# Second layer of a mixture of graph experts: dense over all nodes, or only over gathered (node, expert) rows

## The chip, the core and the metric

The kernel runs on one core of one Trainium2 chip. The metric is the device time of one execution in microseconds (us); smaller is better. The engines named below are PE (TensorE: matmuls, with PEld for its weight loads), DVE (VectorE), ACT (ScalarE), POOL (GpSimd) and SP (SyncE, which here only issues DMAs). All matmuls of the large products take numbers of type fp32r; a float32 operand is cut into a high part (a copy to fp32r) and a low part (the operand less the high part), and a product is then made of two or three matmuls.

## What is computed

N = 1250 nodes, D = 512, 21250 edges, 4 experts of 2 layers, each node takes its best 2 experts.

```python
h = maximum(layernorm(x), 0)
x = x + attention(h, edges, W, b_w, a, b_a)        # h @ W, exp(leaky_relu(s_dst + s_src)), weighted mean over edges
h = maximum(layernorm(x), 0)
gates = softmax(h @ gate_W + gate_b); top_v, top_i = top_k(gates, 2)
def sage_conv(h, W_l, b_l, W_r):
    aggr = segment_sum(h[src], dst) * inv_deg
    return aggr @ W_l + b_l + h @ W_r
for e in range(4):
    g = h
    for l in range(2):
        g = relu(sage_conv(g, Wl[e, l], bl[e, l], Wr[e, l]))
    expert_outs.append(g)
x = x + sum over the node's 2 experts of top_v * expert_outs
```

For the inputs that are run, the four experts are chosen by 54, 917, 1049 and 480 nodes (2500 pairs).

## The kernel before

Nodes are cut into T = 10 tiles of P = 125. `CT` holds the matrix of edge counts (source node in the partitions, 10 tiles; destination in the columns), made from the edge lists by one-hot matmuls. `three(...)` (L1163 to L1169) is the product of two cut operands: high by high, high by low, low by high. Each engine has its own program, in the order written, and waits on semaphores; SP's program is the order of nearly all DMAs.

1. Counts and first product (`tile_and_batch`): one-hot matmuls into `CT`, and `h @ W` by tiles, whose result is cut into `nat_hi` and `nat_lo`; POOL makes the products for the attention's dot products.
2. Attention, 5 steps q of Q = 250 destinations, in each 10 steps s over source tiles: DVE makes `z_c` (L1012, add and clip) and `z_l` (L1019, leaky relu), ACT the exponential `z_e`, DVE `p_f` = `z_e` times counts (L1029), ACT `p_hi`, POOL `p_lo` (L557) and the running sum `p_sum` (L562, L565), PE two products by `three` into the banks of the two destination tiles. `attended(q)` on DVE divides, adds to `xs` and takes the statistics.
3. Second layernorm and gate logits: per tile ACT makes `h2_f`, `nat_hi`, PE turns it (4 transposes, L1282), ACT and DVE cut it into `h2T_hi` and `h2T_lo`, PE makes 12 matmuls of 4 columns for the logits; DVE also makes `CT_hi`.
4. First aggregation, in turned layout (L1308 to L1327): per 250 destinations 10 matmuls for the degrees and 4 x 20 of 250 columns; DVE divides (`ag_f`), ACT and POOL cut it into `agT_hi` and `agT_lo`.
5. `phase1`, per expert e: first layer (`layer1`) of all nodes, weights stationary, 96 matmuls of each block of 500, 500 and 250 nodes; then second layer (`layer2`) of all nodes, *before* the aggregation: `y` = he @ Wl and `r` = he @ Wr + b, 24 matmuls of 512 columns for each of 10 tiles. Both are stored to DRAM (`y_d`, `r_d`). Weights come by 1 MB loads and are cut by ACT and POOL.
6. `phase2`: per expert and destination tile 20 matmuls of 512 columns sum the rows of `y` over the edges (`sum_of`, L1389 and L1399; counts and `y` were loaded again from DRAM and `y` cut again), then DVE `m_f`, ACT `m_g` (gate and relu), POOL `acc` += `m_g`. The sum over the edges thus runs over all 4 experts and all 10 tiles.

Nearly all DMAs go out from SP, and those of tiles span 125 partitions; the weight loads span 128. `beyond` is a flag for counts that fp32r can't hold exactly; it is 0 here, and what stands in its branches does not run.

Of the kernel before, what the change touches and what calls it, by code (L numbers as in the profile page):

```python
# [37 lines left out]
def gnn_kernel(nc, x, src, dst, W0, b_w, a_vec, b_a, gate_W, gate_b, Wl, bl, Wr, out):  # L38
# [20 lines left out]
    assert N == NW * W and NW == T * BW and WT <= 512 and NE == 4  # L59

# [5 lines left out]
    with ctx:  # L66
# [12 lines left out]
        def keep(name, shape, dt):  # L79
            size = 1  # L80
            for n in shape[1:]:
# [6 lines left out]
        rest = keep("rest", [P, T, 250], F32R)  # L88
        rest_raw = at("rest_raw", [P, T, 250], F32, R5)
        row_at = o5[0]  # L90
# [3 lines left out]
        ones_r = keep("ones_r", [P, 128], F32R)  # L94
# [11 lines left out]
        b1 = keep("b1", [128, NE, KC], F32)  # L106
        b1_e = keep("b1_e", [128, KC], F32)
        flag_i = keep("flag_i", [1, 4], I32)
        lg = keep("lg", [P, T, NE], F32)
        lg_s = keep("lg_s", [P, T, NE], F32)  # L110
        lg_e = keep("lg_e", [P, T, NE], F32)
# [4 lines left out]

        he_f = at("he_f", [128, 2, 4 * P], F32, R5)
        b2_b = at("b2_b", [P, D], F32, R5 + 4000)
# [61 lines left out]
        Q = 2 * P  # L180
        slot_at = (RA * Q * 4 + 31) // 32 * 32
        z_c, z_l, z_e, p_f = (at(n, [P, RA, Q], F32, R2 + k * slot_at)
                              for k, n in enumerate(("z_c", "z_l", "z_e", "p_f")))
        p_hi, p_lo = (at(n, [P, RA, Q], F32R, R2 + k * slot_at) for k, n in ((4, "p_hi"), (5, "p_lo")))
        p_sum = at("p_sum", [P, Q], F32, R2 + 6 * slot_at)
        den = at("den", [P, 2], F32, R2 + 32160)
        rden = at("rden", [P, 2], F32, R2 + 32192)
        assert 6 * slot_at + 2 * Q * 4 <= 32160
# [7 lines left out]
        h2_f = at("h2_f", [P, RA, D], F32, R3)  # L196
        gw_f = at("gw_f", [128, KC, NE], F32, R3 + 10240)
        gw_hi = at("gw_hi", [128, KC, NE], F32R, R3 + 10304)
        gw_lo = at("gw_lo", [128, KC, NE], F32R, R3 + 10368)
        prod_src = at("prod_src", [P, D], F32, o5[0])  # L200
        ag_f = keep("ag_f", [128, 2, Q], F32)
        diag_out = keep("diag_out", [P, P], F32)
        assert o5[0] <= 212800, o5[0]
# [138 lines left out]

        def f32(ap):
            return ap.bitcast(F32)

        BLOCKS = [range(0, 4), range(4, 8), range(8, T)]
        GRP = len(BLOCKS) * KC
        QN = N // Q  # L350
        CONSTS = 10
        STORED = 32
# [1077 lines left out]
```

## Time and profile before

| | us |
|---|---|
| median of 3 runs (1095.84 to 1096.91) | 1096.07 |
| span of the profiled execution | 1093.4 |
| PE busy | 909.4 (83%) |
| DVE busy | 426.7 (39%) |
| POOL busy | 333.9 (31%) |
| ACT busy | 259.6 (24%) |
| DMA: 84.03 MB moved, mean | 77 GB/s |

The profiled execution has a span of 1093.4 us between its first and last instruction, 2.7 us below the median of the runs. The page has the busy time of each engine, the same in 40 slices, and groups of instructions by line. A matmul's own duration includes its way through the pipeline: matmuls follow each other faster than they last, so their pace is read from the times at which they start.

### The profile page before, as it was taken

What the parts mean: (1) busy time and instruction counts of PE and PEld (TensorE: products, weight loads), DVE (VectorE), ACT (ScalarE), POOL (GpSimd) and SP (SyncE); (2) the same over time, 40 slices, a digit from 0 to 9 for tenths busy, and PEclk for the clock granted to TensorE, in tenths of its full rate; (3) what the DMA queues carried; (4) which work ended last, traced back from release to release, by engine and by line L of the source; (5) the groups of instructions that cost most, each with busy time, mean ns of one, the idle gap of its engine ahead of it and who ended that gap; (6) DMA issues with size and microseconds to landing.
All of it is one profiled execution on the core that took longest, in us unless ns stands there. A gap on an engine that the chain in (4) does not pass through costs nothing. (4 is left out here: it accounts for less than half of the span.)

```text
span 1093.4 us, 13833 instructions
## 1 busy us (share of the span) xinstructions
PE 909.4 (83%) x4272; PEld 745.7 (68%) x4273; DVE 426.7 (39%) x952; ACT 259.6 (24%) x476; POOL 333.9 (31%) x284
## 2 busy tenths in 40 slices
PE   0068877887999899999999999989995444899997
PEld 0056755665999688887888788868883333678775
DVE  7999979996523711101111111111112001432521
ACT  0134445444511311121012201221112000322321
POOL 7214346875312411044104500450110000222232
PEclk9998898988589999999999999999997666899999
DMA  4100000000142212231322141122223333322212
GB/s 128 39 1 0 0 1 1 1 0 37 67 187 110 87 60 93 76 124 40 112 75 91 47 137 57 51 91 94 90 68 123 131 130 119 133 114 87 114 61 100
DMA packets 38514, 84.03 MB, mean 77 GB/s; under 512 B 4272, under 2 KB 10522, under 8 KB 37601
## 3 DMA queue, kind: packets, MB, share of 16 engines
q1 hardware_dynamic: 38476, 83.51, 21.5%
q8 instruction: 25, 0.41, 0.2%
q14 instruction: 13, 0.11, 0.0%
HBM read 51.66 MB, written 31.85 MB: 76 GB/s over the span
## 5 line engine op out<-in xcount | busy, mean ns | idle before, releaser
L610 POOL TENSOR_TENSOR heT_lo<-he_f,heT_hi 128x500 fp32r<-128x500 f32 (+1 forms) x48 | 51.4, 1083 | 283.4 <-DVE he_f L1116 283.4
L1167 PE MATMUL ps<-W_hi,heT_hi 128*125 128x512 f32 x320 | 128.7, 402 | 9.0 <-POOL heT_lo L610 9.0
L1168 PE MATMUL ps<-W_lo,heT_hi 128*125 128x512 f32 x320 | 127.8, 400 | 0.0
L1169 PE MATMUL ps<-W_hi,heT_lo 128*125 128x512 f32 x320 | 127.5, 398 | 0.0
L639 POOL TENSOR_TENSOR acc<-acc,m_g x40 | 51.4, 1285 | 224.1 <-ACT m_g L814 165.4
L1389 PE MATMUL ps<-y_hi_even,CT 125*125 125x512 f32 x200 | 59.0, 448 | 57.5 <-DMA CT<-ct_hi_d 50.4
L1116 DVE TENSOR_SCALAR he_f<-ps,b 128x500 f32<-128x500 f32 (+1 forms) x48 | 30.9, 651 | 189.6 <-ACT heT_hi L774 169.0
L1124 DVE TENSOR_TENSOR r_s<-ps,b_b 125x512 f32<-125x512 f32 x40 | 27.7, 692 | 192.6 <-PE ps L1169 192.6
L1148 DVE SCALAR_TENSOR_TENSOR m_f<-ps,inv_deg,r_in 125x512 f32<-125x512 f32 x40 | 30.0, 749 | 168.0 <-DMA r_in<-r_d 86.8
L1389 PEld LDWEIGHTS ps<-y_hi_even,CT 125*125 125x125 f32 x200 | 41.8, 211 | 71.4 <-issue 59.5
L599 POOL TENSOR_TENSOR W_lo<-W_raw,W_hi 128x2048 fp32r<-128x2048 f32 x14 | 64.3, 4615 | 53.5 <-ACT W_hi L648 53.5
L1167 PEld LDWEIGHTS ps<-W_hi,heT_hi 128*125 128x125 f32 x320 | 60.4, 189 | 26.6 <-issue 12.1
L814 ACT ACTIVATE m_g<-m_f,gates 125x512 f32<-125x512 f32 x40 | 28.9, 723 | 208.4 <-DVE m_f L1148 155.1
L1167 PE MATMUL ps<-agT_hi,W_hi 128*128 128x500 f32 (+1 forms) x192 | 68.4, 356 | 5.3 <-DVE W_lo L1085 5.3
L1169 PEld LDWEIGHTS ps<-W_hi,heT_lo 128*125 128x125 f32 x320 | 60.4, 189 | 15.5
L1168 PEld LDWEIGHTS ps<-W_lo,heT_hi 128*125 128x125 f32 x320 | 60.6, 189 | 14.4
L1168 PE MATMUL ps<-agT_lo,W_hi 128*128 128x500 f32 (+1 forms) x192 | 68.2, 355 | 0.0
L1169 PE MATMUL ps<-agT_hi,W_lo 128*128 128x500 f32 (+1 forms) x192 | 68.1, 355 | 0.0
L1168 PE MATMUL ps<-h2T_lo,W_hi 128*128 128x500 f32 (+1 forms) x192 | 67.8, 353 | 0.0
L1167 PE MATMUL ps<-h2T_hi,W_hi 128*128 128x500 f32 (+1 forms) x192 | 67.7, 353 | 0.0
L1169 PE MATMUL ps<-h2T_hi,W_lo 128*128 128x500 f32 (+1 forms) x192 | 67.4, 351 | 0.0
L774 ACT ACTIVATE heT_hi<-ps,b_e 128x500 fp32r<-128x500 f32 (+1 forms) x48 | 28.5, 607 | 156.2 <-PE ps L1169 156.2
(199 smaller groups left out, 1830.0 us busy)
## 6 DMA issues: line engine op xcount, KB each, us to landing
y_d<-y_s SPq DMA_DIRECT2D x40, 250.0 KB
r_d<-r_s SPq DMA_DIRECT2D x40, 250.0 KB
r_in<-r_d SPq DMA_DIRECT2D x40, 250.0 KB
W_raw<-in_L_gnn_Wl SPq DMA_DIRECT2D x8, 1024.0 KB, 8.4
W_raw<-in_L_gnn_Wr SPq DMA_DIRECT2D x8, 1024.0 KB, 10.4
ct_hi_d<-CT_hi SPq DMA_DIRECT2D x1, 6103.5 KB
CT<-ct_hi_d SPq DMA_DIRECT2D x5, 1220.7 KB
y_raw_odd<-y_d SPq DMA_DIRECT2D x2, 2500.0 KB
```

What stands on the lines that cost most here:

```text
L599: g.tensor_tensor(lo[:, c, :], W_raw[:, k % 2], f32(hi[:, c, :]), ALU.subtract).then_inc(w_lo_ready.sem, 1)
L610: g.tensor_tensor(heT_lo[:, c, 0:n], he_f[:, c % 2, 0:n], f32(heT_hi[:, c, 0:n]), ALU.subtract).then_inc(he_lo_ready.sem, 1)
L639: g.tensor_tensor(tile, tile, m_g[:, bass.ds(t & 1, 1), :].rearrange("p o d -> p (o d)"), ALU.add).then_inc(acc_ready.sem, 1)
L774: a.activation(heT_hi[:, c, 0:n], ps[:, (0, 1, 6, 7)[c], 0:n], ACT.Relu, bias=b1_e[:, c:c + 1]).then_inc(he_hi_ready.sem, 1)
L814: a.activation(m_g[:, t % 2, :], m_f[:, t % 2, :], ACT.Relu, scale=gates[:, t, bass.ds(e, 1)]).then_inc(m_g_ready.sem, 1)
L1116: v.tensor_scalar(he_f[:, c % 2, 0:n], ps[:, (0, 1, 6, 7)[c], 0:n], b1[:, bass.ds(e, 1), c], 0.0, ALU.add, ALU.max).then_inc(he_f_ready.se ...
L1124: v.tensor_tensor(r_s[:, t % 2, :], ps[0:P, 4 + t % 2, :], b2_b[:], ALU.add).then_inc(rs_ready.sem, 1)
L1148: v.scalar_tensor_tensor(m_f[:, t % 2, :], ps[0:P, t % RB, :], inv_deg[:, t:t + 1], r_in[:, t % RB, :], ALU.mult, ALU.add).then_inc(m_f_re ...
L1167: mm(o, l_hi, r_hi, start=start, stop=False)
L1168: mm(o, l_hi, r_lo, start=False, stop=False)
L1169: return mm(o, l_lo, r_hi, start=False, stop=stop)
L1389: mm(o, CT2[:, j, n], y_hi[i][:, j], start=j == 0, stop=False)
```

## The change

All parts come at once.

- Attention in pairs of source tiles: every operation but the exponential and its argument runs on two tiles (500 elements). The argument is one operation (`max(0.2 * row + ..., row + ...)` by way of `row_low`, `s_rest` and a bias `s_low` of the exponential) in place of two. POOL has no part left; `p_sum` and `p_lo` go to DVE. PE also turns the counts (20 transposes of 125 columns per q), ACT copies them out with their row sums (the degrees), and SP stores them to `c_d`, a [N, N] matrix with destinations as rows.
- First aggregation in natural layout: counts stationary, features moving, 10 x 10 x 2 matmuls of 512 columns, in two halves of 5 destination tiles; the first half runs between layernorm, transposes and logits. The logits take 8 matmuls of 8 columns per tile. The means are turned afterwards (40 transposes).
- First layer in natural layout: nodes stationary, weights moving, 24 matmuls of 512 columns per tile and expert, experts in the order 2, 3, 0, 1. DVE adds the bias, ACT takes relu and high part, DVE the low part; SP stores the hidden rows raw (`t_d`) and cut (`he_d`), and the cut second weights (`w2_d`). ACT issues the weight loads.
- Pairs: marks of the chosen experts, their running numbers (one product with a triangle of ones), tables and records are made on DVE in the first expert's time; POOL scatters the records by 20 indirect DMAs and reads them back. Each expert's pairs fill tiles of 128, 23 tiles in all, whatever the inputs.
- Second layer per tile of 128 pairs: POOL gathers the rows of `c_d` (5000 bytes each) and of `t_d` (2 KB each); PE turns the count rows, sums the hidden rows over the edges (20 matmuls of 512), turns mean and hidden rows, and multiplies by the second weights (24 of 512); DVE and ACT add the bias, gate; POOL adds the rows to `out` by an accumulating indirect DMA. Hidden rows and weights of the next expert (9.3 MB) are loaded by SP into the other half of `slots`.
- Stores and loads of 125 partitions are cut into 112 and 13 (`CUTS`).

```diff
-    RA = 5
+    RA = 3
+    NP = T // 2
+    S = 128
+    NT = (2 * N - NE) // S + NE
+    PO = (1, 2, 3, 0)
+    LE = (2, 3, 0, 1)
...
+        CUTS = (slice(0, 112), slice(112, P))
...
+            def store_group(x, g):
+                for t in GROUPS[g]:
+                    sp.wait_ge(*pre_ready(x * T, t + 1))
+                    n = (x * T + t) % 4
+                    for m in CUTS:
+                        sp.dma_start(t_d[LE[x], m, t, :], he_t[m, n, :]).then_inc(t_out[n].sem, 16)
+                    if x < NE - 1:
+                        sp.wait_ge(*he_lo_ready(x * T, t + 1))
+                        for m in CUTS:
+                            sp.dma_start(he_d[LE[x], t, m, :], f32(HE[m, t, :])).then_inc(he_out.sem, 16)
...
+            for i in range(NT):
+                if i + 3 < NT:
+                    pool.wait_ge(*crow_turned(3 * (i + 1)))
+                    gather_counts(i + 3)
+                if i + 3 < NT and i >= 1:
+                    pool.wait_ge(*hrow_used(i))
+                    gather_hidden(i + 3)
+                if i > 0:
+                    pool.wait_ge(*out_stored(16 * i))
+                pool.wait_ge(*tg_ready(i + 1))
+                add_sum(i)
...
+            for g in range(NP * QN + 2):
+                if g < NP * QN:
+                    arguments(g)
+                if 1 <= g <= NP * QN:
+                    weights(g - 1)
...
+                if g >= 2:
+                    sum_up(g - 2)
+                    weights_low(g - 2)
+                if g > NP and g % NP == 3:
+                    attended(g // NP - 1)
...
+            for t in range(T):
+                pe.wait_ge(*h2_lo_ready(t + 1))
+                pe.wait_ge(*ct_hi_ready(t + 1))
...
+                neighbours1(t, 0)
+                logits(t)
+                if t + 2 < T:
+                    turn2(t + 2)
+            for t in range(T):
+                neighbours1(t, 1)
...
+            for x in range(NE):
+                for g, tiles in enumerate(GROUPS):
+                    for t in tiles:
+                        last = half(x, g, t, 0)
...
+                    for t in tiles:
...
+                        half(x, g, t, 1).then_inc(l1_done.sem, 1)
...
+            for i in range(NT):
+                k, he_here, w2_here = slot_of(i)
+                if i > 0:
+                    turn_hidden(i)
+                neighbours(i, k, he_here)
+                if i + 1 < NT:
+                    turn_rows(i + 1)
+                if i == 0:
+                    turn_hidden(i)
+                turn_means(i)
+                transformed(i, k, w2_here)
```

## Rows read from the trace of the kernel before

**Rows 1.** Page: granted TensorE clock in 40 slices, tenths of full speed.
```profile
PEclk9998898988589999999999999999997666899999
```

**Rows 2.** Windows by stage: length, busy time (instructions), granted clock, DMA share, GB/s.
```profile
0.00:165.70 165.70, 86.91 (x430) 69.24 (x431) 147.14 (x481) 53.01 (x129) 65.22 (x57) 0.94 0.10 28
165.70:262.50 96.80, 82.72 (x315) 59.94 (x316) 90.93 (x174) 46.54 (x107) 74.98 (x95) 0.91 0.00 0
262.50:303.50 41.00, 34.06 (x167) 33.44 (x165) 22.79 (x52) 19.45 (x32) 13.10 (x10) 0.54 0.23 92
303.50:364.50 61.00, 55.70 (x451) 55.40 (x451) 21.50 (x33) 12.22 (x24) 13.70 (x20) 0.95 0.30 122
364.50:822.80 458.30, 449.31 (x2112) 371.12 (x2112) 75.23 (x134) 78.49 (x105) 115.52 (x62) 0.99 0.25 83
822.80:945.50 122.70, 60.35 (x210) 44.92 (x209) 22.14 (x29) 16.57 (x29) 10.41 (x9) 0.73 0.33 127
945.50:1093.40 147.90, 140.35 (x592) 111.65 (x592) 47.00 (x53) 33.31 (x52) 40.96 (x32) 0.96 0.26 98
```

**Rows 3.** Waits of PE: for whom, us in total, times, longest.
```profile
PE ps L1389 <- DMA CT<-ct_hi_d: 50.4, 4, 21.9
```

**Rows 4.** Chain that ended last: start, us, what; two blocks of ten matmuls.
```profile
953.62 2.32 PE ps L1399 x10
955.94 2.32 PE ps L1389 x10
```

**Rows 5.** Timeline of PE at the full and at the half clock: start, us, what.
```profile
71.38 0.40 PE L1232 MATMUL ps<-W_hi,hT_lo 128*125 128x512 f32 x1
71.61 0.59 PE L1206 MATMUL ps<-ident,h_f 125*128 125x125 f32 x4
72.04 3.08 PE L1195 MATMUL ps<-onehot_g,onehot_p 125*125 125x250 bf16 x25
...
302.17 0.35 PE L1167 MATMUL ps<-gw_hi,h2T_hi 128*125 128x4 f32 x1
302.37 0.35 PE L1168 MATMUL ps<-gw_lo,h2T_hi 128*125 128x4 f32 x1
```

**Rows 6.** Instructions that touch z_c: duration min/median/max in ns.
```profile
L1019 DVE SCALAR_TENSOR_TENSOR z_l<-z_c x50: 401/414/955, 166.2 to 254.5; 125x250 f32<-125x250 f32 x50
```

**Rows 7.** Groups by line: shapes, count, busy us, mean ns, idle before.
```profile
L1049 DVE CAST CT_hi<-CT 125x1250 fp32r<-125x1250 f32 x10 | 11.2, 1122 | 1.2 <-issue 1.2
L732 ACT ACTIVATE h_f<-xs,shift,rstd 125x512 f32<-125x512 f32 x10 | 7.9, 804 | 0.5 <-DVE shift L900 0.5
L1001 DVE SCALAR_TENSOR_TENSOR xs<-ps,rden,xs (+1 forms) x10 | 7.0, 746 | 1.1 <-DVE rden L996 1.1
L1051 DVE TENSOR_TENSOR h2T_lo<-ps,h2T_hi 128x500 fp32r<-128x500 f32 x10 | 6.7, 671 | 1.0 <-ACT h2T_hi L648 1.0
L1005 DVE BATCH_NORM_STATS2 x_stats<-xs (+1 forms) x10 | 6.4, 680 | 0.0
L648 ACT ACTIVATE h2T_hi<-ps 128x500 fp32r<-128x500 f32 x10 | 5.9, 587 | 10.1 <-PE ps L1282 10.1
L1057 DVE TENSOR_TENSOR lg<-ps,gb_b 125x4 f32<-125x4 f32 x10 | 1.6, 163 | 14.7 <-PE ps L1169 14.7
```

**Rows 8.** Windows in weight loads (128 partitions) and in loads of 125 partitions.
```profile
414.00:417.00 3.00, 3.00 (x15) 2.49 (x14) 0.43 (x1) 0.68 (x1) 0.00 (x0) 1.00 1.00 331
...
485.00:488.00 3.00, 3.00 (x15) 2.47 (x14) 0.00 (x0) 0.00 (x0) 0.00 (x0) 1.00 1.04 383
...
880.00:890.00 10.00, 5.72 (x14) 4.46 (x15) 0.00 (x0) 0.00 (x0) 0.00 (x0) 0.50 0.34 134
```

**Rows 9.** Timeline of the last microseconds, and SP's last wait.
```profile
1085.89 0.75 DVE L1148 SCALAR_TENSOR_TENSOR m_f<-ps,inv_deg,r_in 125x512 f32<-125x512 f32 x1 [3.89 <-PE ps L1399]
1086.72 0.72 ACT L814 ACTIVATE m_g<-m_f,gates 125x512 f32<-125x512 f32 x1 [3.92 <-DVE m_f L1148]
...
SPq L66 <- DMA out<-acc: 3.6, 1, 3.6
```

More of the change, by code:

```diff
@@ L504, in link @@
                 pool.wait_ge(*pool_step(step[0]))
[L506 to L507 removed]
+            pool.sem_inc(hw_lo_ready.sem, hw_lo_ready.start)
             link(g.memset(ident[:], 0.0))
@@ new lines, in hidden @@
+            def hidden(x, g):
+                for t in GROUPS[g]:
+                    act.wait_ge(*pre_ready(x * T, t + 1))
+                    if x > 0:
+                        act.wait_ge(*he_out(32 * x * T))
+                    a.activation(HE[:, t, 0:D], he_t[:, (x * T + t) % 4, :], ACT.Relu).then_inc(he_hi_ready.sem, 1)
+            for i in range(4):
+                mean1(i)
+            mean1_high(0)
+            mean1(4)
+            for i in range(1, 5):
+                mean1_high(i)
@@ L1032, in _, with columns, arguments @@
-            weights(0, False)
-            with dve.Fori(1, QN) as q:
-                weights(q, True)
+                    dve.wait_ge(*x2_ready(q * 2 + i + 1))
+                    v.bn_stats(x_stats[:, q * 2 + i, :], xs[:, q * 2 + i, :]).then_inc(stats_ready.sem, 1)
+            def columns(g):
+                return slice(g // NP * Q, (g // NP + 1) * Q)
+            def arguments(g):
+                n = g % RA
+                if g >= RA:
+                    dve.wait_ge(*ze_ready(g + 1 - RA))
+                for m in range(2):
+                    s = g % NP * 2 + m
+                    last = v.scalar_tensor_tensor(z_l[:, n, m, :], row[0:P, columns(g)], s_rest[:, s:s + 1],
+                                                  row_low[:, columns(g)], ALU.add, ALU.max)
+                last.then_inc(zl_ready.sem, 1)
@@ new lines, in _ @@
+            for x in range(NE):
+                if x > 0:
+                    cut_low(x, 1)
+                hidden(x, 0)
+                if x == 0:
+                    places()
+                    tables()
+                    records()
+                    dve.wait_ge(*fields_ready(1))
+                hidden(x, 1)
+                cut_low(x, 2)
+                cut_low(x, 3)
+                if x < NE - 1:
+                    cut_low(x + 1, 0)
+                hidden(x, 2)
+            dve.wait_ge(*rec_in(16))
@@ new lines, in part, with turn_hidden @@
+            def part(k, row, first, n):
+                return slots[0:n, bass.ds(k, 1), first:first + D].rearrange("p o d -> p (o d)")
+            def turn_hidden(i):
+                pe.wait_ge(*hrow_in[i % 4](16 * (i // 4 + 1)))
+                if i > 0:
+                    pe.wait_ge(*heT_lo_ready(i))
+                for c in range(KC):
+                    last = nc.tensor.transpose(ps[:, 3, c * S:(c + 1) * S], hrow[i % 4][:, c * 128:(c + 1) * 128],
+                                               ident[:])
+                last.then_inc(hrow_used.sem, 1)
```

1416 lines of the change are left out of this document (823 added, 593 removed).

## The prediction

> **What bounds the kernel now.** I read the windows by stage first. Six stages follow each other: counts and first product to 165.7 us, attention to 262.5, second layernorm and logits to 303.5, first aggregation to 364.5, the experts' products to 822.8, and the sums over edges to the end at 1093.4. In four of the seven windows (the last stage is two) PE is busy 85 to 98% of the time [rows 2]; as busy time includes the pipeline, pace is the better sign. In the chain ten matmuls of 512 columns take 2.32 us, 0.232 us each [rows 4]: that is PE at the full clock with nothing between. Phase 2 holds 800 such matmuls, 186 us of its 270.6; the rest is its first 122.7 us, where PE is busy 60.4 us, the granted clock is 0.73 and DMA moves 127 GB/s [rows 2], 50.4 us of waiting for four loads of counts among it [rows 3]. The stage from 262.5 to 303.5 has a clock of 0.54 [rows 1, 2]: small matmuls, and a chain of ACT, PE and DVE. In attention DVE is busy 90.9 of 96.8 us with POOL at 75.0 beside it [rows 2]. So the end is set by the count of PE's large matmuls, by DVE in attention, and by DMA at the head of phase 2.
>
> **DMA.** Loads of 125 partitions run at 134 GB/s with a share of 0.34 of the 16 engines; weight loads of 128 partitions fill them (share 1.00 and 1.04) at 331 and 383 GB/s [rows 8]. So a transfer of 125 partitions uses 5 of 16 engines, about 27 GB/s each. The change cuts such transfers into 112 and 13 partitions; no row shows 112. The bounds are the two rows, 134 and 383 GB/s. I take 330, since 112 is a multiple of 16 and 125 is not, and 128 goes at that.
>
> Against this edit the Trainium skill ("DMA: Bandwidth & Descriptors", Rules for kernel authors) says of two transfers to disjoint partition halves not to bother, as they serialize; by that the experts' stage would be the DMA rival below. The same page (Why a DMA increments its semaphore by 16 and not by 1) has the engines used as the largest number up to 16 that divides the slowest dimension, which gives 5 for 125, as the 0.34 shows, 16 for 112 and 13 for 13; I hold with this one.
>
> **Part by part**
>
> *Counts and first product*: nothing of weight changes; four small bias loads go from SP's queue, where nobody waits for them. 165.7 us stay.
>
> *Attention.* DVE per pair of source tiles: two arguments of 0.414 us (the median of the same operation on 250 elements, most of it undisturbed [rows 6]), and weights, sum and low part on 500 elements, each as the 0.671 of a 500 element operation [rows 7]: 0.83 + 2.01 = 2.84 us, 25 times 71 us. `attended` costs 2 x 0.746 + 2 x 0.680 + about 0.3 = 3.2 us [rows 7], four times inside the loop: 13. With the scaled row 85 us. The mean durations of today include POOL's use of memory beside DVE (one operation has 401 ns at least and 955 at most [rows 6]); POOL is idle afterwards. PE: 300 x 0.232 = 70 us, 100 transposes for `c_d`, and sums. A transpose of 125 columns at the full clock takes 0.43/4 = 0.11 us (four from 71.61, next work at 72.04 [rows 5]), so 11 us: 82 us in all. Two engines at 82 and 85 us that hand tiles to each other through three buffers, with ACT behind both, won't reach either bound; today 96.8 stand over 90.9 busy ones [rows 2], and I add 7: 92 us. Bounds 86 and 99. End at 257.7. The low part moves from POOL to DVE, behind the sum in its queue: both are in the 85 us. The stores to `c_d` (6.3 MB, SP and DMA idle here [rows 2]) cost nothing; the same holds for POOL's removed part.
>
> *The gap before the aggregation.* PE then waits for the last `attended` (2.9 us of large operations), statistics, one `CT_hi` (1.1 us), the degrees and the first low part (0.7) [rows 7]; with some ten small operations of 0.16 us and the handovers, 7 us, in which the clock can fall; 2 us more for its return, up to 4 (today's aggregation, begun at the half clock, lies in a slice of 0.8 before one of 0.9 [rows 1]). Begin at 266.7.
>
> *Layernorm, logits and first half of the aggregation together.* PE per tile: 10 x 0.232 = 2.3 us, 8 logit matmuls at 0.1 (they start 0.20 us apart at the half clock [rows 5]; I take half of that), 4 transposes at 0.11: 3.6 us. DVE per tile: `CT_hi` 1.12 at most, two low parts of 0.67: 2.5. ACT: 0.80 + 2 x 0.59 = 2.0 [rows 7]. PE decides: 36 us. *Second half*: 100 x 0.232 + 5 means turned at 0.44 = 25.5, with waits 26. The first layer starts at 328.7, where it starts at 364.5 now: 35.8 us gained up to here.
>
> *First layer.* 4 x 10 x 24 matmuls x 0.232 = 222.7 us; today its turned form costs about the same. Added on PE: 20 transposes (2.2). DVE per expert: bias and low part 10 x 1.4, weights' low parts 16 x 0.67: 25 of 55.7 us. ACT has as many instructions less the bias. For the first expert DVE also makes places, tables and records between its first and second group: some 80 chained small operations at 0.16 plus the handover, say 0.25 (none hidden within DVE): 20 us. Eight banks and four buffers hold PE's results meanwhile, and the next expert's weights, cut behind this, are due 55 us in and come at about 55: cover just enough; 1 us. DMA per expert: hidden rows 5.1 + 2.6 MB, second weights out 4.2 MB, weights in 4.2 MB, 16.1 MB; at 330 GB/s 49 us, under PE's 55.7. The stores queue on SP behind each other only. A weight load is issued from ACT behind ACT's waits for the last cut; it has 16 us until it's needed and takes 3 at 383 GB/s [rows 8]. With 1 us for the rest: 227 us, end at 555.7. The 20 scatters of records on POOL, at the 3.6 us of a last store [rows 9] each, are 72 us under some 150 us of cover.
>
> *Second layer.* Per tile of 128 pairs on PE: 20 + 24 matmuls of 512 = 10.2 us, and 10 + 4 + 4 transposes x 0.11 = 2.0: 12.2 us. Handovers: the mean (ACT, 0.6) is covered by the 1.1 us of turning the next count rows; its high and low part (0.59 + 0.67) by the 2.8 us of the product with the hidden rows. DVE 3.7 us and ACT 3.1 per tile by the same rows. The register loads at a tile's head are not on the path if PE's queue holds work: today's batches load eight values behind the matmuls of 71.38 and the transposes start 0.23 us after [rows 5]. 23 x 12.2 = 281 us, for 222 + 271 today: 960 matmuls of `layer2` and phase 2. At the head 5 us (the last hidden rows are stored, then gathered, behind the 5.7 us of sums and count rows). At the end bias and gate 0.75 + 0.72, and the scatter, nearest to the 3.6 us of the last store [rows 9], taken with its read as 5: 7 us. Together 293 us, end at 848.7.
>
> *Gathers.* No row shows an indirect DMA. Per tile 0.64 + 0.26 + 0.26 MB, the last moved twice: 1.42 MB, and 9.3 MB of the next expert per 4 to 9 tiles. If all goes at 330 GB/s: the tightest is the expert of 54 pairs, loaded in the 49 us of the one of 480 (4 tiles): 9.3 + 4 x 1.42 = 15 MB, 45 us: fits. If the indirect ones go at the 134 of 125 partitions: 10.6 us per tile, still under 12.2, but on engines that the loads use too. Gathers are issued three tiles ahead, the accumulates wait only for each other. I take them at nothing.
>
> By themselves: the Trainium skill (same page, Anatomy of one DMA) gives a DMA from POOL 2.0 us plus bytes at 436 GB/s, by which the three would take 3.5, 2.6 and 2.6 us; no row bears on it.
>
> **The sum.** 165.7 + 92 + 9 + 36 + 26 + 227 + 293 = 848.7 us of span; with the 2.7 us between span and median, 851. The saving is about 245 us: 5 + 31 before the first layer, 209 from 5000 rows of the second layer down to 2944 and from the stalls at the head of phase 2.
>
> **Rivals**
>
> 1. *The clock stays at half in layernorm and first half* (chance 0.12). It did at 0.54 with small matmuls [rows 2]. For it: 12 of 22 instructions per tile are small. Against: the ten large ones fill most of the time, and the aggregation of today rose to 0.95. Price: 36 us become 72: 887.
> 2. *DMA sets the pace* (0.15). If 112 partitions also go over 5 engines, hidden rows alone take 7.7 MB / 134 GB/s = 57 us, and with a share of the other 8.4 MB about 80 per expert for three experts: +73, 924. If only the indirect ones do, they share five engines with the loads: 32.7 MB at 134 is 244 us, loads a further 27.9 MB / 330 = 85: 329 for 281, 899. If the rate is 330 but stores and loads disturb each other (250 GB/s), 64 per expert: +25, 876.
> 3. *Handovers cost in each tile* (0.10): one uncovered pair of ACT and DVE, 1.5 us x 23 = 35: 886.
> 4. *Slower than before* (0.03): POOL's making of the descriptors. It builds 384 rows per tile, in series. To pass 1096 a tile must take 12.2 + 10.7 = 22.9 us, 60 ns per row; at 75 ns, 29 us per tile, 1234 us. Nothing in the profile speaks for it but that SP's issues are small and POOL's unknown. That the count of tiles is not reduced is excluded: it is fixed at 23.
>
> **How the numbers follow.** My forecast 851 (its own bounds 86 to 99 in attention, 5 to 12 at the gap and some us in each stage: 835 to 872) has 0.60. Below 830 would need the gap, the coupling and the head gone. The range 830 to 915 leaves out the first of rival 2 (0.05), two rivals at once and rival 4. A measurement can tell about 0.2% from no change. Faster: all but rival 4, 0.96; same 0.01; slower 0.03.
>
> **What would show it.** `z_l` by pairs with DVE busy over 90% of attention and PE's first expert matmul near 329; clock 0.9 or more from 270 on; 24 matmuls per tile 5.6 us, wl and l1 without waits for `HE` or stores; starts of the tiles of pairs 12.2 us apart, and the DMA share in stores near 0.9. Wrong it would be by a clock of 0.5 in 267 to 303, a PE wait for `W1`, `he_t` or `slots` of tens of us, tiles over 13 us apart or waits for gathered rows.

## The result and the profile after

| | before | changed |
|---|---|---|
| time, median | 1095.95 us (1095.49 to 1096.91, 4 runs) | 861.39 us (859.00 to 863.82, 4 runs) |
| ratio | | 0.7857, 95% interval 0.7841 to 0.7873 |
| profiled execution | span 1093.4 us | span 862.1 us, mean granted clock 0.973 |

The change takes 21% off the time. The forecast was 851 us in a range of 830 to 915: inside, 10.4 us too low.

The page of the changed kernel gives PE's share, the granted clock and the share of the DMA engines in 40 slices (rows 1 are the clock of before):

```profile
PE 752.3 (87%) x3620; PEld 611.0 (71%) x3621; DVE 444.7 (52%) x1088; ACT 254.6 (30%) x516; POOL 176.2 (20%) x160
...
PEclk9999899889997999999999999999999999999997
DMA  4200000011124014769989695369934993449910
```

The stretch at 0.5 to 0.6 of [rows 1] (layernorm) and the one at 0.6 to 0.7 (head of phase 2) are gone. What is left of low clock is one dip behind the attention. The windows by stage, with the columns of [rows 2] (length, busy time of PE, PEld, DVE, ACT, POOL with counts, granted clock, DMA share, GB/s), for attention, the gap, the first and the second half of the aggregation, the first layer by expert, the second layer, and the tail:

```profile
165.70:260.80 95.10, 88.14 (x433) 72.56 (x434) 75.14 (x157) 53.93 (x141) 0.00 (x0) 0.94 0.20 64
260.80:267.40 6.60, 2.11 (x17) 1.67 (x16) 5.41 (x16) 6.08 (x10) 0.00 (x0) 0.91 0.56 186
267.40:304.50 37.10, 37.09 (x198) 32.01 (x199) 17.91 (x29) 12.32 (x22) 0.00 (x0) 0.88 0.21 64
304.50:332.20 27.70, 27.70 (x136) 22.49 (x135) 7.50 (x21) 10.41 (x19) 0.00 (x0) 1.00 0.08 30
332.20:389.00 56.80, 56.80 (x259) 45.66 (x258) 37.80 (x137) 18.37 (x34) 16.73 (x25) 1.00 0.67 211
389.00:445.00 56.00, 53.21 (x222) 41.95 (x221) 20.18 (x33) 13.73 (x25) 13.57 (x11) 0.97 0.86 275
445.00:501.00 56.00, 56.00 (x242) 44.53 (x241) 22.93 (x38) 14.94 (x27) 0.00 (x0) 1.00 0.82 292
501.00:566.30 65.30, 63.66 (x279) 50.56 (x278) 25.21 (x41) 14.21 (x25) 1.97 (x2) 1.00 0.60 204
566.30:850.70 284.40, 281.15 (x1416) 232.62 (x1414) 84.51 (x137) 57.30 (x92) 77.74 (x66) 1.00 0.65 187
850.70:862.10 11.40, 0.02 (x1) 0.00 (x0) 0.69 (x1) 0.72 (x1) 1.55 (x1) 0.61 0.01 0
```

The spans differ by 231 us: 32 of them were gained before the first layer starts (332.2 for 364.5), 199 behind. Read PE against the length: from 267.4 to 850.7 it idles for 7.7 of 583 us, 5.7 of them in the last three waits below. From 276.6 on the bound is the number of PE's large matmuls at the full clock, nearly everywhere. PE's waits from the gap on (who is waited for, us in total, times, longest), which stand for the 50.4 us of [rows 3]:

```profile
PE ps L1579 <- DVE nat_lo L1183: 4.4, 1, 4.4
PE ps L1417 <- DVE W L1220: 2.8, 1, 2.8
PE ps L1641 <- DMA crow<-c_d,rec: 1.6, 1, 1.6
PE ps L1685 <- DMA hrow<-t_d,rec: 1.3, 1, 1.3
```

The gathers and the scatter had no row in the trace of before. Here they are groups of POOL (count, busy us, mean ns of one, idle before), two from the page and one from the groups of the second layer's window:

```profile
L611 POOL DMA_INDIRECT out<-tg,rec x23 | 36.9, 1605 | 192.3 <-ACT tg L877 175.5
L601 POOL DMA_INDIRECT crow<-c_d,rec x23 | 22.4, 976 | 150.1 <-PE ps L1419 143.4
```

```profile
L601 POOL DMA_INDIRECT hrow<-t_d,rec x23 | 21.9, 952 | 18.7 <-DMA t_d<-he_t 12.0 <-issue 6.7
```

POOL needs 3.5 us per tile of 12.25 for all three; most of its idle time is waiting for the finished tile.

### The profile page after: what moved, and what is told of

Same layout as the page of the kernel before. It is cut to its first block, busy times and chain, and to the rows that moved or that the text cites. A ratio compares the mean times of both kernels' runs of the same rounds, so it can differ in the third digit from the quotient of the medians.

```text
span 862.1 us, 11919 instructions
## 1 busy us (share of the span) xinstructions
PE 752.3 (87%) x3620; PEld 611.0 (71%) x3621; DVE 444.7 (52%) x1088; ACT 254.6 (30%) x516; POOL 176.2 (20%) x160
## 4 chain that ended last, share of the span: by engine, by line
PE 71%; DVE 18%; DMA 4%; issue 3%; DVEq 1%; ACT 1%; POOL 0%; POOLq 0%; SPq 0%; ACTq 0%
PE ps L1417 15%; PE ps L1419 15%; PE ps L1418 15%; PE ps L1714 6%; PE ps L1713 5%; DVE onehot_g L1025 5%; PE ps L1579 3%; DVE column L1013 3%; PE ps L1580 3%; PE ps L1641 3%; DMA raw<-in_L_gnn_Wr 2%; DVE onehot_p L966 2%; PE ps L1685 1%; PE ps L1724 1%; PE ps L1510 1%
## 5 line engine op out<-in xcount | busy, mean ns | idle before, releaser
L1714 PE MATMUL ps<-slots,CTs 125*128 x230 | 90.9, 395 | 0.0
L1713 PE MATMUL ps<-slots,CTs 125*128 x207 | 81.6, 394 | 0.0
L1417 PE MATMUL ps<-W,h2T_hi 128*125 128x512 f32 x160 | 64.2, 401 | 2.8 <-DVE W L1220 2.8
L1418 PE MATMUL ps<-W,h2T_hi 128*125 128x512 f32 x160 | 63.8, 399 | 0.0
L1419 PE MATMUL ps<-W,h2T_lo 128*125 128x512 f32 x160 | 63.7, 398 | 0.0
L1417 PE MATMUL ps<-W,agT_hi 128*125 128x512 f32 x160 | 63.6, 397 | 0.0
L1419 PE MATMUL ps<-W,agT_lo 128*125 128x512 f32 x160 | 63.3, 396 | 0.0
L1418 PE MATMUL ps<-W,agT_hi 128*125 128x512 f32 x160 | 63.2, 395 | 0.0
L1445 PE MATMUL ps<-onehot_g,onehot_p 125*125 125x250 bf16 x250 | 45.3, 330 | 18.1 <-DVE onehot_g L1025 15.3
L1025 DVE TENSOR_SCALAR onehot_g<-iota_h,column 125x250 bf16<-125x250 f16 x250 | 49.6, 281 | 2.2 <-DVE column L1013 2.2
L1714 PEld LDWEIGHTS ps<-slots,CTs 125*128 125x128 f32 x230 | 43.2, 188 | 9.6
L1417 PE MATMUL ps<-nat_hi,p_hi 125*125 125x512 f32 x100 | 43.6, 436 | 7.1 <-DVE p_lo L1128 7.1
L1579 PE MATMUL ps<-nat_hi,CT_hi 125*125 125x512 f32 x100 | 42.7, 427 | 4.4 <-DVE nat_lo L1183 4.4
L1713 PEld LDWEIGHTS ps<-slots,CTs 125*128 125x128 f32 x207 | 38.8, 187 | 9.4
```

The costliest lines, as they stand in the source:

```text
L1025: last = v.tensor_scalar(onehot_g[:, k, j, :], iota_h[:], column[:, k, j:j + 1], None, ALU.is_equal)
L1417: mm(o, l_hi, r_hi, start=start, stop=False)
L1418: mm(o, l_hi, r_lo, start=False, stop=False)
L1419: return mm(o, l_lo, r_hi, start=False, stop=stop)
L1445: last = mm(ps[0:P, k, 0:WT], onehot_p[:, bass.ds(first + j, 1), :].rearrange("p o n -> p (o n)"), onehot_g[:, slot, j, :], start=opens an ...
L1579: mm(o, count, nat_hi[:, t, :], start=t == 0, stop=False)
```

## The experiments

Median times are to be held against 861.39 us; a ratio is always to the kernel before, measured beside it. A time given without a ratio or a range is of one execution. The executions of one and the same part differ: the attention ends at 259.7 to 260.9 us in the nine kernels, the changed one among them, that have it in the same form, and the loop of layernorm and aggregation takes 62.0 to 64.8 us where its form is the same.

### The cut of the hidden rows' transfers

Does the pace of the first layer really hang on 112 partitions? Two other cuts of the same bytes:

```diff
-        CUTS = (slice(0, 112), slice(112, P))
+        CUTS = (slice(0, 115), slice(115, P))      # first run
+        CUTS = (slice(0, 100), slice(100, P))      # second run
```

> The changed kernel (861.4 us) with its tiles cut into 115 and 10 partitions in place of 112 and 13; same number of DMAs and bytes. Theory of the engines' number: 115 is divided by 5 and by nothing larger up to 16, so these transfers run on 5 of 16 DMA engines at about 134 GB/s as those of 125 partitions did before; hidden rows of an expert are 7.7 MB, of which 92% are in the large pieces, 53 us and with the share of the other 8.4 MB some 75 to 80 us per expert against 56 on PE: the first layer ends 50 to 80 us later, the time is 910 to 950 us, and the DMA share stays near 0.33 to 0.5 in the stores. Rival (what limits is only a piece of fewer than 128 partitions, or bytes): no change, 860 us.

> The transfers of hidden rows are cut into 100 and 25 partitions instead of 112 and 13. Theory (a transfer goes over as many engines as the largest number up to 16 that divides its rows: 10 for 100, 5 for 25): per expert the ten busiest engines carry at least 0.62 MB of hidden rows and 0.53 MB of the rest each, at some 27 GB/s 42 to 54 us of the 56; the first layer becomes 0 to 15 us longer, the time 861 to 880 us, far below the 957.4 of the cut at 115, and the mean DMA share in the first layer stays near 0.8. Rival (what matters is that the second part is small and the first near 128, not the divisor): with 100 the time would lie no lower than the 957 of the cut at 115.

Measured: 957.43 us with 115, 885.24 us with 100. Windows in the first layer, two of each, of the kernel cut at 115, then at 100, then at 112:

```profile
456.00:464.00 8.00, 3.29 (x15) 2.27 (x13) 2.97 (x5) 2.39 (x6) 0.00 (x0) 1.00 0.43 127
...
484.00:496.00 12.00, 10.11 (x43) 8.07 (x44) 4.23 (x7) 2.59 (x5) 0.00 (x0) 1.00 1.01 358
```

```profile
436.00:448.00 12.00, 8.81 (x38) 6.67 (x36) 7.43 (x13) 6.15 (x12) 0.00 (x0) 1.00 0.59 200
...
460.00:472.00 12.00, 9.56 (x42) 7.32 (x41) 3.19 (x5) 2.19 (x4) 0.00 (x0) 1.00 1.01 378
```

```profile
444.00:460.00 16.00, 16.00 (x70) 12.69 (x69) 6.08 (x10) 3.50 (x7) 0.00 (x0) 1.00 1.02 377
472.00:480.00 8.00, 8.00 (x36) 6.39 (x35) 2.29 (x4) 1.01 (x2) 0.00 (x0) 1.00 1.04 409
```

Each kernel has full stretches (share 1.01 to 1.04), in which weights of 128 partitions move as well, and the first two have plateaus: 127 GB/s with 115, 200 GB/s with 100. At the 27 GB/s per engine of the prediction that is 4.7 and 7.4 engines. The kernel cut at 112 shows no plateau in these stretches. Where it moves hidden rows alone, as the 127 GB/s with 115 are, it reaches 281 GB/s:

```profile
437.00:440.00 3.00, 3.00 (x15) 2.38 (x13) 3.00 (x6) 3.00 (x7) 0.00 (x0) 1.00 0.91 281
```

PE's waits with 115:

```profile
PE ps L1417 <- DVE he_t L1252: 34.7, 3, 14.9
...
PE ps L1417 <- DVE W L1220: 24.3, 5, 9.3
...
PE ps L1699 <- DMA slots<-he_d: 11.7, 1, 11.7
```

The first layer takes 308 us instead of 234: the +73 of rival 2 in its first form, measured as +74, and the second layer another 20 us. The waits look like DVE's, but DVE waits for buffers that the stores hold. The cut at 100 falls between (its 885 us lie 5 above the expected range: 12.0 us of waits for `W`, 3.9 for `he_t`, and clock lost with them). So with neither of the two other cuts does the first layer stay PE's, and it is not the size of the large part that decides, since 112 lies between them. The Trainium skill ("DMA: Bandwidth & Descriptors", Why a DMA increments its semaphore by 16 and not by 1, at "How many engines (k)") takes the largest number up to 16 that divides the slowest dimension, 5, 10 and 16 for these three; the trace agrees in order, with rates somewhat under 5 and 10 engines' worth; the shares of 0.43 and 0.59 are 6.9 and 9.4 of 16 engines. The same page's advice (Rules for kernel authors) not to bother with two transfers to disjoint partitions holds for halves that each reach all engines; here the choice of the split is worth 96 us.

### Layernorm and aggregation in one loop, or apart

```diff
             for t in range(T):
-                neighbours1(t, 0)
                 logits(t)
                 if t + 2 < T:
                     turn2(t + 2)
+            for t in range(T):
+                neighbours1(t, 0)
```

> The changed kernel with the first half of the aggregation taken out from between the logits: PE first turns all ten tiles and makes all logits, then the 100 matmuls of the first half. Theory: the interleaving hid a chain of ACT, PE and DVE of 2 to 3.7 us per tile behind PE's matmuls; apart, the logits take 25 to 37 us at the half clock (as the 41 us of the stage before, at 0.54) and the first half 23 us more: the first layer starts 20 to 35 us later, 880 to 895 us. Rival (the gain came from the natural layout alone, 46 us of matmuls for 56): under 10 us later.

Measured: 872.06 us. The small matmuls are alone again; both windows, logits and aggregation:

```profile
267.40:290.70 23.30, 22.91 (x112) 22.88 (x113) 16.89 (x28) 11.93 (x21) 0.00 (x0) 0.50 0.26 74
290.70:341.60 50.90, 50.90 (x222) 40.74 (x223) 7.49 (x21) 10.65 (x19) 0.00 (x0) 0.95 0.07 21
```

Granted clock 0.50 for all 23.3 us, the half level, as in the 0.54 of [rows 2]; the first layer starts at 341.6 instead of 332.2. So rival 1's mechanism is real and the interleaving keeps it away, but it is worth some 10 us, less than expected. From the end of the attention to the first layer it is 102 us before (262.5 to 364.5), 82 when apart (259.8 to 341.6; the attention ended 1.0 us earlier in this execution) and 71 when woven (260.8 to 332.2). The larger part, 20 us, comes with the other logits and the layout of the aggregation. It was no chain of engines that went away: the kernel before has PE busy in 33.3 of the 34.4 us of its logits, at the half level too, with 160 small instructions for 112:

```profile
269.10:303.50 34.40, 33.27 (x160) 32.82 (x160) 18.44 (x32) 18.31 (x30) 13.10 (x10) 0.50 0.25 98
```

### The gap before the aggregation

The large matmuls begin at the half clock: they stand 0.43 us apart up to 276.4 and 0.23 after. 18 matmuls whose result nobody reads fill PE's gap:

```diff
+            for k in range(18):
+                mm(ps[0:P, 5, :], nat_hi[:, T - 1, 0:P], nat_hi[:, T - 1, :], ...)
             pe.wait_ge(*gw_lo_ready(1))
```

> The changed kernel with 18 matmuls of 512 columns without use, into a free bank, in the gap of 4.4 us ahead of the aggregation, whose first 9 us ran at the half clock (pairs 0.43 us apart for 0.23). Theory: the clock stays at the full level over the gap, PE starts at 267.5 at 0.23 us per matmul and reaches the first layer 3 to 4 us earlier: 857.5 to 858.5 us. Rival: the extra work delays the first matmul by as much, or ACT and DVE decide the first tiles' pace: no change, 861 us.

Measured: 857.42 us (855.47 to 861.92), ratio 0.7817 (0.7784 to 0.7849). PE in this kernel:

```profile
261.69 4.44 PE L1597 MATMUL ps<-nat_hi 125*125 125x512 f32 x18
266.36 0.47 PE L1579 MATMUL ps<-nat_hi,CT_hi 125*125 125x512 f32 x1 [0.23 <-issue]
266.66 0.39 PE L1580 MATMUL ps<-nat_lo,CT_hi 125*125 125x512 f32 x1
266.89 0.39 PE L1579 MATMUL ps<-nat_hi,CT_hi 125*125 125x512 f32 x1
```

The large ones stand 0.23 us apart at once, and the first layer starts at 326.9, 5.3 us earlier. Of that 1.0 us is no gain of the edit: in this execution the attention had ended 1.0 us earlier. The loop itself takes 60.5 us instead of 64.8, 4.2 less. The forecast had put 2 us on this return of the clock. Against the 62.0 to 64.8 us that the loop takes in the executions without the edit it is worth 1.4 to 4.2.

### The weight load behind the large store

`W_r` of the next expert is asked for at 385.65 and cut at 403.40 (timeline of ACT: the issue, then the cut with the idle time before it), with the window between the two:

```profile
385.65 0.38 ACTq L798 DMA_DIRECT2D raw<-in_L_gnn_Wr  x1
...
403.40 1.15 ACT L648 ACTIVATE W<-raw 128x512 fp32r<-128x512 f32 x2 [11.26 <-DMA raw<-in_L_gnn_Wr]
```

```profile
385.70:403.40 17.70, 16.31 (x70) 12.62 (x68) 3.79 (x6) 1.91 (x4) 14.26 (x12) 1.00 1.01 310
```

17.7 us for 1 MB, while the engines are full (1.01, 310 GB/s): it shares them with what SP has issued, above all the 4.2 MB store of the second weights, issued at 380.96. PE's wait of 2.8 us for it ends at 404.8, and soon after the clock falls too (timeline of PE):

```profile
406.43 0.63 PE L1417 MATMUL ps<-W,h2T_hi 128*125 128x512 f32 x1
406.85 0.63 PE L1418 MATMUL ps<-W,h2T_hi 128*125 128x512 f32 x1
```

Seven matmuls stand 0.43 us apart before the 0.23 returns at 409.7, 1.4 us more. In the other kernel that store comes one group later:

```diff
                 store_group(x, 1)
+                if x < NE - 1:
+                    store_group(x, 2)
                 sp.wait_ge(*w_lo_ready(KC * (cut_number(x, 3) + 1)))
                 if x < NE - 1:
                     sp.dma_start(w2_d[LE[x]]...)      # 4.2 MB
-                store_group(x, 2)
+                    store_group(x, 2)                 # last expert, as before
```

> The changed kernel with SP storing the second weights (4.2 MB) after the third group's hidden rows and not before them. The load of the first layer's right weights for the second expert took 17.7 us (issued at 385.65, cut from 403.4 on) and PE waited 2.8 us for it, while the DMA share was 0.94 to 1.04. Theory: the 4.2 MB store issued 5 us before it fills the same engines; behind it the load lands in 8 to 12 us and PE's wait for W is gone: 3 to 4 us faster, 857 to 859 us. Rival: the engines are as full then by the other stores, or ACT waits longer for the second weights' buffer in turn: no change or slower, 861 us or more.

Measured: 856.60 us (855.51 to 859.19), ratio 0.7804 (0.7788 to 0.7820). The same load is cut at 392.06, 6.4 us after its issue, at a DMA share of 0.77:

```profile
392.06 2.18 ACT L650 ACTIVATE W<-raw 128x512 fp32r<-128x512 f32 x4
```

PE's wait for `W` is gone and the first layer ends 4.7 us earlier: the 2.8 of the wait, the 1.4 of the clock, and half a microsecond. In the six other executions of kernels that leave the stores as they are and do not gather twice the first layer takes 229.8 to 234.3 us, in the three that store late 229.2 to 229.4: what the edit is worth differs from execution to execution, up to 5 us.

How the load came to be late is seen in the packets of the two queues. From its issue to 390.0 not one of its packets moves, while SP's queue moves 1.43 MB. Then, in the 8 us from 391 on (queue q1 is SP's, q10 ACT's; packets, MB, share of the engines):

```profile
q1 hardware_dynamic: 496, 1.72, 66.5%
q10 hardware_dynamic: 478, 0.96, 31.2%
```

The Trainium skill ("DMA: Bandwidth & Descriptors", Queues, rings and completion order) says that an engine serves the queues it has work for in turn, packet by packet. These 8 us agree, with as many packets of one queue as of the other; SP's are the larger, so most of the rate is SP's. It does not explain the 4.3 us after the issue in which the load does not move at all, nor that its last 34 of 528 packets come between 399.0 and 403.4; both stay open. With the late store its first packets move within 1.3 us.

### Attention: PE or DVE?

First 70 of the 100 transposes of the counts are left out (with them most of the count table that the second layer gathers from):

```diff
-                for k in range(n):
+                for k in range(1):
                     last = nc.tensor.transpose(ps[0:P, 6 + r % 2, ...
```

> Leaves out 70 of the 100 transposes of the counts matrix between the attention steps, so most of the table of neighbour counts stays unwritten and the output is not the reference's. In the changed kernel one attention step takes 17.6 us from step to step, VectorE is busy in 75 of the stage's 95.1 us and TensorE in 88. Theory (TensorE sets the pace of the attention and the transposes lie in its row): 70 transposes of about 0.1 us go, the stage becomes 6 to 8 us shorter, and the time 853 to 856 us. Rival (the chain VectorE, ScalarE, VectorE sets it, as my forecast had it with VectorE 85 us): TensorE gets idle time instead, the stage stays within 2 us of 95, and the time is 859 to 863 us.

Measured: 853.93 us (850.93 to 857.37), ratio 0.7801 (0.7782 to 0.7820). The aggregation starts at 261.25 instead of 267.40, and an attention step takes 16.7 us instead of 17.6: 0.9 of the 14 x 0.11 = 1.5 us that PE was spared per step. So PE sets the pace of the attention in the changed kernel, and a little more than half of what it is spared arrives. What holds the rest was not tested; PE's waits in the stage for `p_lo` of DVE grow, and the chain of DVE and ACT is the likely one. Second, the running sum and the low part go back to POOL:

```diff
-                    v.tensor_tensor(p_sum[:], p_sum[:], p_f[:, n], ALU.add)       # DVE's queue
-                v.tensor_tensor(p_lo[:, n], p_f[:, n], f32(p_hi[:, n]), ALU.subtract)
+                    g_.tensor_tensor(p_sum[:], p_sum[:], p_f[:, n], ALU.add)      # POOL's queue
+                g_.tensor_tensor(p_lo[:, n], p_f[:, n], f32(p_hi[:, n]), ALU.subtract)
```

> The running sum of the weights and the low half of each weight tile go back from VectorE to GpSimd, as in the kernel before; all else as changed. They are 50 operations of 0.67 us on VectorE, 33.6 us of its 75 in the stage. Theory (GpSimd's two operations per pair, at the length they had in the kernel before, fill more than the 3.5 us that a pair now has): the attention stage becomes 10 to 30 us longer, paced by GpSimd, and the time 871 to 890 us. Rival (GpSimd has room, TensorE goes on setting the pace): 17.6 us per step stay, VectorE is busy for some 42 us instead of 75, and the time is 859 to 863 us.

Measured: 858.05 us (856.08 to 858.29), ratio 0.7829 (0.7816 to 0.7842), 3.3 us below the changed kernel, the intervals just touching; both expectations missed part of it. The arguments `z_l` in the changed kernel, then here (minimum/median/maximum in ns), and two groups of DVE here (busy us, mean ns):

```profile
L1094 DVE SCALAR_TENSOR_TENSOR z_l<-row,s_rest,row_low x50: 460/471/478, 165.1 to 248.7; 125x250 f32<-125x250 f32 x50
```

```profile
L1121 DVE SCALAR_TENSOR_TENSOR z_l<-row,s_rest,row_low x50: 465/478/1487, 165.3 to 246.2; 125x250 f32<-125x250 f32 x50
```

```profile
L1121 DVE SCALAR_TENSOR_TENSOR z_l<-row,s_rest,row_low 125x250 f32<-125x250 f32 x50 | 44.2, 925 | 0.1
L1136 DVE SCALAR_TENSOR_TENSOR p_f<-z_e,CT 125x500 f32<-125x500 f32 x25 | 27.2, 1086 | 1.7 <-ACT z_e L740 1.7
```

With POOL idle all 50 arguments take 0.46 to 0.48 us. With POOL at work half of them do, and others up to 1.49. The mean rises from 0.471 to 0.925, that of the weights from 0.674 to 1.086 us: 50 x 0.454 + 25 x 0.412 = 33 us. The operations moved away are 45 (20 sums and 25 low parts, not the 50 of the expectation), 45 x 0.672 = 30 us. DVE gives back in waiting what it is spared in work: it is busy 82.2 us of the stage, for 75.1 in the changed kernel. The step takes 17.1 us instead of 17.6. The Trainium skill ("SBUF — State Buffer", SBUF: two separate sides) has DVE operations with two inputs in SBUF and POOL's that read SBUF exclude each other for a whole instruction; the durations agree (half of them 0.48 us or less, the others with a wait on top, in all up to 1.49). So moving these operations to DVE, as the change does, gains nothing by itself; it costs. In the three executions with them on POOL (this and the two under "The gains together") the attention ends at 257.6 to 258.3 us, against 259.7 to 260.9.

### The second layer: gathers, scatter, tiles

A second gather of the count rows per tile, issued when the first has landed:

```diff
             def gather_counts(i):
+                gather(crow[i % 3][:], c_d, i, 0, first_in)
+                pool.wait_ge(*first_in(16 * (i + 1)))
                 gather(crow[i % 3][:], c_d, i, 0, crow_in[i % 3])
```

> Each gather of a tile's count rows (112 to 125 rows of the counts table) is made twice, the second after the first has landed, so one more indirect gather with its landing, some 1 us of GpSimd and 2 to 3 us of waiting, stands on GpSimd for each of the 23 tiles. Theory (the gathers lie beside 12.2 us of matmuls per tile and are hidden): 12.25 us from tile to tile stay, only the first tile starts 2 to 4 us later, time 861 to 866 us. Rival (the hand-over of each tile, gathers, turning and evicting, is near the pace): 2 to 4 us more per tile, time 905 to 950 us.

Measured: 895.05 us, between the two. POOL in this kernel (timeline; idle before and its releaser in brackets), in a stretch with loads for the next expert and in a quiet one, and the windows around them:

```profile
631.54 0.94 POOL L602 DMA_INDIRECT crow<-c_d,rec  x1 [11.75 <-DMA crow<-c_d,rec]
...
749.74 0.98 POOL L602 DMA_INDIRECT crow<-c_d,rec  x1 [0.30 <-issue]
...
756.44 0.94 POOL L602 DMA_INDIRECT crow<-c_d,rec  x1 [5.71 <-DMA crow<-c_d,rec]
```

```profile
600.00:634.00 34.00, 27.82 (x129) 22.76 (x128) 7.49 (x12) 4.99 (x8) 6.37 (x6) 0.90 1.03 316
726.00:760.00 34.00, 34.00 (x175) 28.34 (x174) 11.05 (x18) 7.49 (x12) 14.34 (x13) 1.00 0.66 182
```

In quiet stretches (share 0.66) a gather lands 5.7 us after its instruction ends, 6.7 after its start, the tiles go at 11.1 us on POOL and PE stays full: all is hidden, even twice. In three bursts (share 1.03 to 1.04), when the next expert's 9.3 MB come in, the landing takes 11 us and more, two tiles each take 17 to 20 us, and PE waits 14.4 us in five waits and drops its clock. A sixth, of 5.9 us, is for the very first count rows, in front of the second layer. That a gather costs nothing because it runs three tiles ahead of its use is the reading of this; no run gathered fewer tiles ahead. The landing of 6.7 us, beside other traffic (share 0.66), stands against the 3.5 us that the prediction worked out for the count rows from the Trainium skill's figures ("DMA: Bandwidth & Descriptors", Anatomy of one DMA); the measurement decides.

A tile less: the 23rd holds padding alone with these inputs.

```diff
-    NT = (2 * N - NE) // S + NE
+    NT = 22
```

> 22 tiles of pairs instead of 23 in the second layer. The 23rd is there for the worst spread of pairs over the four experts; with this spread (9, 8, 4 and 1 tiles) it holds padding alone, and the output stays the reference's. Theory (TensorE's 12.25 us per tile are the pace of the second layer, gathers, evictions and scatters lie beside it): 12.3 us less, 848 to 851 us. Rival (part of the stage's time is tied to something that does not shrink with the tiles, such as the loads of the next expert's weights): less than 8 us gained, 853 us or more.

Measured: 849.89 us (846.89 to 851.96), ratio 0.7735 (0.7718 to 0.7752): 11.5 us less. The scatters stand 12.25 us apart in both kernels. The last scatter now has rows to write (10.65 us from its start to the end, 8.94 with padding), which takes 1.7 off the gain; the rest of the difference is between executions (this one reaches the second layer 3.0 us earlier, and has six matmuls at the half level there, which the other has not).

A scatter that writes instead of adding:

```diff
-                                     bounds_check=N - 1, oob_is_err=False, compute_op=ALU.add
+                                     bounds_check=N - 1, oob_is_err=False
```

> The scatter of each finished tile writes its rows instead of adding them to what lies there, so the residual and the other expert's share are left out of the output. Per tile nothing should change by either theory: 12.25 us from tile to tile. Theory (the end after the last matmul is made of a read, an addition and a write in memory): the 7.4 us between the end of the last scatter's instruction on GpSimd and the end of the span become 3 to 5 us, and the time is 857 to 859 us. Rival (the landing of any indirect write at the end takes that long): 7 to 8 us stay, time 860 to 862 us.

Measured: 859.54 us (856.93 to 861.18), ratio 0.7834 (0.7815 to 0.7853): no difference to be told. POOL's instruction takes 1.0 instead of 1.6 us, and 7.3 us still follow it (7.4 before), as the rival had it. This run tells less than was meant: the last tile is padding, so in both kernels nothing is left to be added at the end. The kernel of 22 tiles shows the tail with real rows, in which its last data moves until 844 us:

```profile
841.00:844.00 3.00, 0.00 (x0) 0.00 (x0) 0.00 (x0) 0.00 (x0) 0.10 (x1) 0.68 0.33 37
844.00:850.20 6.20, 0.00 (x0) 0.00 (x0) 0.00 (x0) 0.00 (x0) 0.00 (x0) 0.50 0.00 0
```

For 6.2 us nothing moves and nothing computes. In the kernel before, data still moves in the last 1.4 us. Whether the addition of real rows is a part of the 1.7 us by which this tail is longer was not tested.

### The gains together

The edits for the gap, the late store and POOL together, then with 22 tiles on top.

> Three edits at once that each gained a little alone: 18 idle matmuls in the gap before the aggregation (857.4 us alone), the second-layer weights stored one group later (856.6 us), the running sum and the low half of the weights on GpSimd (858.1 us). Theory (they sit in three different stages, and the gains add): 861.4 - 4.0 - 4.8 - 3.3 = 849 us, 847 to 852. Rival (the small gains are partly the same one: the clock's dips or the state of a run): 853 to 857 us.

> The three edits of the run before and 22 tiles instead of 23. If all four gains add, 861.4 - 4.0 - 4.8 - 3.3 - 12.3 = 837 us, 835 to 840; if the three small ones overlap, 841 to 845 us.

Measured: 852.32 us (852.04 to 853.48), ratio 0.7769 (0.7756 to 0.7782), and 841.85 us (841.69 to 843.17), ratio 0.7670 (0.7657 to 0.7683). Both lie above the sums of the single gains (849 and 837): the first at the edge between the two expectations, the second on the rival's side. A part of each single gain was spread between runs, 859.0 to 863.8 for the changed kernel itself. By the trace the three edits each do their part: the aggregation starts at 264.35, the first layer at 324.89, the first count rows are turned at 550.28 instead of 562.12, and no wait for `W` is left. The last kernel takes 2.3% less than the changed one, 10.5 us of it only by the spread of these inputs over the experts: it would be wrong for the spreads that need the 23rd tile.

## Why the prediction was right, and where it was off

| step | predicted | measured | difference |
|---|---|---|---|
| end of attention | 257.7 | 260.8 | +3.1 |
| gap | 9 | 6.6 | -2.4 |
| both halves of the aggregation | 62 | 64.8 | +2.8 |
| first layer | 227 | 233.9 | +6.9 |
| second layer up to the last matmul | 286 | 284.6 | -1.4 |
| tail | 7 | 11.4 | +4.4 |
| span | 848.7 | 862.1 | +13.4 |

The profiled execution was one of the slower ones; its span is 0.7 us above the median, where 2.7 us had been added. That is why the span is 13.4 us off and the time 10.4. The path was right and several terms were not; that two of the six errors have the other sign is luck.

**Right.** The path: PE's large matmuls at 0.232 us, 12.25 us per tile (12.2 predicted), 56 us per expert. The transfers of 112 partitions near the rate of 128 (281 GB/s alone, 377 and 409 with weights), on which the 73 us of rival 2 hung, and the same price by experiment. Clock at full in the woven loop from 276.6 on (a clock of 0.9 from 270 on had been named as the sign). Gathers and scatters hidden, at 3.5 us of POOL per tile. The saving of 231 us in the span was forecast as 245: 36 and 209 where 32 and 199 came.

**Attention: right sum, wrong engine.** The step named DVE (85 us) ahead of PE (82). Busy is PE 88.1 and DVE 75.1 of 95.1 us, 79% where over 90% had been named as the sign. DVE's sum was made of full durations, and these do add up to 86 us; but operations in a row overlap, as DVE's timeline in the changed kernel shows (start, duration: 0.67 long, 0.59 apart):

```profile
213.86 0.67 DVE L1109 SCALAR_TENSOR_TENSOR p_f<-z_e,CT 125x500 f32<-125x500 f32 x1
214.45 0.67 DVE L1121 TENSOR_TENSOR p_sum<-p_sum,p_f 125x500 f32<-125x500 f32 x1
215.04 0.67 DVE L1128 TENSOR_TENSOR p_lo<-p_f,p_hi 125x500 fp32r<-125x500 f32 x1
```

0.07 us in each of 157 instructions make the 11 us between 86 and 75. (The sum also had 25 running sums where the kernel has 20.) The run with fewer transposes shows PE as the pace; the one with POOL shows that the move to DVE gains nothing and costs 1 to 3 us. What the step left out is the start: PE's first matmul comes at 171.46, after a wait of 5.9 us, and its first 13 stand 0.43 us apart, which costs 2.6 us. The 7 us added by judgement covered most of this.

**Gap and clock: mis-sized both ways.** 7 + 2 us were put down; 6.6 us of gap came, and then 9 us at half pace, a loss of about 4 us, which is in the row of the aggregation. The idle matmuls took 4.2 off the loop.

**First layer: one wrong term.** "It has 16 us until it's needed and takes 3 at 383 GB/s": the load took 17.7. The rate came from a window in which weights moved alone [rows 8]; the step's own sum of 16.1 MB in 55.7 us had the engines near full, and there a load shares them. Cost: 2.8 us of wait and 1.4 of the clock behind it; by the run with the later store 4.7, within a spread that reaches from nothing to 5. The rest is transposes, the turning of the first count rows, which runs before the last matmuls of the layer, and the wait of 1.6 us for them.

**Tail: mis-sized.** Bias, gate and the scatter of 5 us "with its read" made 7; it took 11.4, of which 8.9 are the scatter. The nearest row was a plain store [rows 9]. What differs is argued to be the form of DMA: no run ended with another. The addition is not what this tail is made of, since its last tile is padding and the writing scatter has a tail as long.

**The rivals.** The first (half clock) exists and is kept away by the interleaving, at some 10 us rather than 36: only the small matmuls would run at half. The second exists as forecast. The third and the fourth did not show: no wait of PE recurs from tile to tile, and POOL takes 8 ns per gathered row (0.976 us for up to 128) against the 60 that would have decided. Two parts of the change have no run of their own: the natural layout of the first layer, and the second layer over gathered rows as such; for the latter the price of a tile (11.5 us by the run with 22) stands in for it.

## What to carry to other kernels

Where transfers are to hide under matmuls, the number of partitions in each decides the rate: cut 125 rows as 112 and 13, never 115 and 10. Price a load by the other traffic in flight, not by its rate alone, and issue a large store behind the small load that PE needs next. Before moving work between VectorE and GpSimd look at the minimum and maximum of the durations: if they differ by about the length of the other's instruction, the move may gain nothing, as here.

## What the runs showed of the hardware

- VectorE's operations with two inputs take 0.46 to 0.48 us beside an idle GpSimd and up to 1.49 us beside a working one; ScalarE's `z_e` stays at 0.50 in both.
- Two queues in work at once moved equal numbers of packets (478 and 496 in 8 us), the load with the smaller packets fewer bytes.
- An indirect gather of up to 128 rows costs GpSimd 0.95 to 0.98 us, an adding scatter 1.6, a writing one 1.0. A gather lands 5.7 us after its instruction ends, and 11 us and more after it when the DMA engines are full.
- Short waits of PE could have an echo in its clock: after the wait of 2.8 us 3 us at the half level (1.2 GHz), after the gap before the aggregation 9 us. Such an echo cost half as much as the wait, or as much. It did not always come: the same wait for `W` was 2.3 us in the kernel with the writing scatter and had one, and was 2.0 us with 22 tiles and 1.8 with POOL and had none.
- The kernels here, which end with an indirect scatter, have about 6 us at their end in which nothing moves. What they are made of stays open: no run took the wait at the end apart, or ended with another form of DMA.
